# Another order of the head steps and another bank table in a gated delta-rule attention kernel

## The reference, cut to what matters

```
qkvz = x @ W_qkvz ; q, k, v go through a causal convolution of 4 taps and silu
q, k are normalised; each of 16 key heads serves 2 value heads (32 in all, width 128)
for every token t, for every value head:
    S = S * exp(g_t);  delta = (v_t - k_t S) * beta_t
    S = S + k_t delta; o_t = q_t S
out = (silu(z) * rms_norm(o) * norm_w) @ W_out
experts: 12 dense experts (256 -> 640 -> 256) with a top-3 mask, then an early-exit factor
```

## Time and profile before

| what | us |
|---|---|
| median of 3 runs (1511.14 to 1515.55) | 1513.2 |
| the profiled execution, its own time | 1513.14 |
| its span in the profile | 1511.4 |
| PE, DVE, ACT, POOL busy in the span | 1422.6, 1129.0, 1060.1, 704.5 |

### The profile page before, as it was taken

One profiled execution on the slowest core, in us unless ns is written; L12 is line 12 of the kernel. 1 busy time (PEld: TensorE's weight loads), 2 busy tenths in 40 slices (PEclk: granted clock), 3 DMA queues, 4 the chain that ended last, 5 costly groups with the idle time before them and its releaser, 6 DMA issues.

```text
span 1511.4 us, 38181 instructions
## 1 busy us (share of the span) xinstructions
PE 1422.6 (94%) x15004; PEld 1133.0 (75%) x15004; DVE 1129.0 (75%) x1992; ACT 1060.1 (70%) x2136; POOL 704.5 (47%) x619
## 2 busy tenths in 40 slices
PE   5679999999999999999999999999877999999995
PEld 3459888897888889888888888888853465665675
DVE  5579999999999999999999999998765421221224
ACT  6467887878788887878888787887646646546430
POOL 0535545455554544555545455544327534435330
PEclk9799999999999999999999999999999899999997
DMA  3000203112020211202021120302330211111100
GB/s 115 1 1 23 57 2 58 23 37 36 23 58 2 58 23 37 36 23 58 9 51 31 29 37 22 57 13 33 69 77 31 70 36 36 59 47 36 36 1 29
DMA packets 101000, 55.92 MB, mean 37 GB/s; under 512 B 74572, under 2 KB 93016, under 8 KB 100824
## 3 DMA queue, kind: packets, MB, share of 16 engines
q1 hardware_dynamic: 100824, 53.47, 14.8%
HBM read 35.62 MB, written 1.05 MB: 24 GB/s over the span
## 4 chain that ended last, share of the span: by engine, by line
PE 70%; DVE 9%; issue 7%; POOL 5%; ACT 5%; DMA 4%; DVEq 0%; SPq 0%; POOLq 0%; ACTq 0%
PE bank L387 8%; PE bank L1327 8%; PE bank L1311 7%; PE bank L542 5%; PE bank L588 4%; PE bank L559 4%; PE bank L529 3%; PE bank L577 3%; PE bank L568 3%; DVE con L878 3%; DMA sqo<-oo 3%; PE bank L469 2%; ACT h L1427 2%; PE bank L477 2%; PE bank L485 2%
## 5 line engine op out<-in xcount | busy, mean ns | idle before, releaser
L878 DVE SCALAR_TENSOR_TENSOR con<-bank,taps,con 128x1022 f32<-128x1022 f32 (+2 forms) x192 | 245.4, 1278 | 13.0 <-ACT con L657 8.4
L1633 POOL TENSOR_TENSOR h<-h 128x512 f16<-128x512 f32 x120 | 147.4, 1231 | 162.6 <-ACT h L1427 155.5
L1034 POOL TENSOR_TENSOR gl<-const_sb,gc 128x512 f16<-128x512 f32 x128 | 129.6, 1039 | 144.2 <-DVE gc L888 84.3
L387 PE MATMUL bank<-x,qkv 128*128 128x512 f16 x768 | 184.5, 392 | 10.8 <-DVE con L878 10.8
L1311 PE MATMUL bank<-y,w 128*128 128x512 f16 x720 | 170.2, 387 | 10.8 <-ACT h L1427 8.1
L1426 ACT ACTIVATE h<-bank,b 128x512 f32<-128x512 f32 x120 | 82.4, 687 | 122.0 <-PE bank L1311 120.2
L1327 PE MATMUL bank<-w,h 128*128 128x256 f16 x1440 | 162.9, 276 | 1.7 <-DVE facc L1542 1.2
L1327 PEld LDWEIGHTS bank<-w,h 128*128 128x128 f16 x1440 | 141.6, 99 | 23.5 <-DVE facc L1542 3.6
L1311 PEld LDWEIGHTS bank<-y,w 128*128 128x128 f16 x720 | 64.1, 99 | 112.1 <-ACT h L1427 47.7
L387 PEld LDWEIGHTS bank<-x,qkv 128*128 128x128 f16 x768 | 73.2, 100 | 93.3 <-issue 12.3
L936 DVE TENSOR_TENSOR X<-X,bank 128x512 f16<-128x512 f16 x192 | 129.6, 682 | 15.2 <-PE bank L477 13.4
(11 more groups left out here) (217 smaller groups left out, 3924.3 us busy)
## 6 DMA issues: line engine op xcount, KB each, us to landing
w<-in_w SPq DMA_DIRECT2D x24, 640.0 KB, 4.5
w_qkv<-in_W_qkvz SPq DMA_DIRECT2D x16, 512.0 KB, 3.9
w_z<-in_W_qkvz SPq DMA_DIRECT2D x16, 256.0 KB, 2.8
w_out<-in_W_out SPq DMA_DIRECT2D x16, 256.0 KB, 3.0
Z<-in_xT SPq DMA_DIRECT2D x2, 512.0 KB, 5.7
y<-in_x SPq DMA_DIRECT2D x1, 1024.0 KB, 8.1
sqo<-oo SPq DMA_TRANSPOSE x64, 3.1
out_dram<-y SPq DMA_DIRECT2D x8, 128.0 KB, 1.8
```

Of the source, the lines that this page charges most:

```text
L387: last = mm(bank[:, b], qkv16[:, w, a, t * P:(t + 1) * P], x16[:, x, a, b * S:(b + 1) * S], start=(a == k == 0), stop=(a == HT - 1 and k = ...
L878: stt(out=out, in0=bank[:, 0:B, 0:S - k], scalar=taps[:, par, t, TAPS - 1 - k:TAPS - k], in1=out, op0=ALU.mult, op1=ALU.add).then_inc(tap_ ...
L1034: last = tt(gl[:, g % 2, k].rearrange("p (m r) d -> p m r d", m=2), upper.unsqueeze(1).unsqueeze(1).broadcast_to([P, 2, R, P]), gc[:, par, ...
L1633: tt(h16[:, n % 3, 1, t, at], h32[:, k % H32], h16[:, n % 3, 0, t, at], ALU.subtract).then_inc(h_low, 1)
```

## The change

ORDER has the same 167 steps in another sequence. Six of them belong to another head relative to the walk: `once`(1), `res`(3) go from a = 0 to 1; `gl`(2), `decay`(0), `decay`(1) from 2 to 1; the load of w_qkv from 2 to 3. BANK is another table. Every instruction keeps its shape and operands. The five bank constants of the gates and the experts change too, and the walk in which the gate steps come last is now named (-2) since the deepest is now -3; that walk holds only the load for head 0, which is issued ahead of the walks in both kernels.

```
-    (1, "kk", 0), (1, "load", "z"), (1, "aT", 0), (1, "kk", 1),
+    (1, "decay", 0), (0, "Z", 2), (1, "kk", 0), (1, "kk", 1),
...
-GATE_BANKS = (4, 2)
+GATE_BANKS = (6, 2)
+GATE_WALK = -2
 DEEP = max(a for a, *_ in ORDER)
...
-    if w > -DEEP:
+    if w != GATE_WALK:
         return ORDER
...
-H_BANKS = (3, 5)
-LOGIT_BANK, SUM_BANK = 4, 6
-O_BANKS = (2, 7)
+H_BANKS = (3, 4)
+LOGIT_BANK, SUM_BANK = 6, 7
+O_BANKS = (5, 2)
```

More of the change, by code:

```diff
@@ L39 @@
 ORDER = [
[11 rows of a table removed]
-    (1, "aH", 3), (2, "load", "qkv"), (1, "turn", (0, 0)), (1, "unit", 3),
[10 rows of a table removed]
[L62 to L67, removed]
@@ L68 @@
-    (1, "y", (5, 0)), (1, "p", (3, 1)), (2, "tap", 2), (2, "sq1", 1),
-    (0, "weigh", 0), (2, "tok", 0), (2, "tok", 1), (1, "turn", (4, 0)),
[5 rows of a table removed]
[L75 to L79, removed]
@@ L80 @@
-    (1, "res", 2), (1, "Z", 0), (1, "once", 2), (1, "kd", 1),
-    (2, "silu", 0), (1, "aL", 3), (0, "op", 2), (2, "decay", 1),
+    (1, "decay", 0), (0, "Z", 2), (1, "kk", 0), (1, "kk", 1),
+    (1, "aT", 0), (1, "gl", 2), (1, "pT", 0), (1, "unit", 0),
+    (0, "split", "z"), (1, "unit", 1), (1, "decay", 1), (0, "Z", 1),
+    (1, "v", (1, 0)), (1, "aT", 1), (0, "solve", 0), (0, "once", 3),
+    (0, "oT", 0), (1, "kk", 2), (1, "pT", 1), (0, "su", 0),
+    (2, "split", "qkv"), (1, "aH", 0), (1, "aL", 0), (1, "decay", 2),
[7 rows of a table added]
@@ new lines @@
+    (1, "load", "out"), (1, "unit", 2), (1, "turn", (0, 0)), (1, "y", (1, 0)),
[6 rows of a table added]
+    (1, "turn", (0, 1)), (1, "p", (2, 0)), (0, "pdl", 2), (0, "sqo", 1),
+    (1, "p", (1, 1)), (1, "y", (3, 0)), (2, "tap", 2), (0, "sum", 1),
+    (0, "sum", 2), (2, "sq1", 1), (2, "tok", 0), (2, "tok", 1),
+    (0, "sqo", 2), (0, "solve", 3), (1, "turn", (2, 0)), (2, "silu", 2),
[6 rows of a table added]
+    (0, "power", 0), (0, "weigh", 0), (1, "turn", (4, 0)), (1, "turn", (3, 1)),
+    (0, "low", 0), (0, "high", 0), (0, "high", 1), (0, "weigh", 1),
@@ new lines @@
+    (1, "y", (4, 1)), (0, "z", 2), (1, "p", (5, 0)), (0, "z", 3),
+    (1, "p", (4, 1)), (2, "tap", 3), (0, "weigh", 2), (1, "turn", (5, 0)),
+    (2, "gl", 0), (2, "v", (0, 0)), (0, "weigh", 3), (1, "load", "z"),
+    (1, "y", (5, 1)), (0, "low", 1), (1, "turn", (4, 1)), (3, "load", "qkv"),
+    (1, "res", 0), (1, "res", 1), (2, "kT", 0), (0, "high", 2),
+    (0, "low", 2), (1, "once", 0), (0, "op", 0), (2, "silu", 3),
+    (0, "low", 3), (0, "high", 3), (2, "proj", 0), (1, "p", (5, 1)),
+    (0, "op", 1), (1, "Z", 0), (1, "kd", 1), (2, "tap", 0),
@@ L82 @@
+    (1, "turn", (5, 1)), (1, "once", 1), (1, "res", 2), (1, "res", 3),
+    (0, "op", 2), (2, "gl", 1), (1, "once", 2), (2, "silu", 0),
     (0, "op", 3),
@@ L85 @@
 BANK = {
[11 rows of a table removed]
-    ("solve", 3): 7, ("turn", (3, 0)): 3, ("decay", 0): 4, ("y", (3, 1)): 2, ("pdl", 3): 7,
-    ("p", (4, 0)): 6, ("turn", (2, 1)): 5, ("norm", 0): 3, ("y", (5, 0)): 4, ("p", (3, 1)): 7,
-    ("tok", 0): 6, ("tok", 1): 5, ("turn", (4, 0)): 2, ("z", 0): 3, ("z", 1): 4,
[3 rows of a table removed]
-    ("once", 0): 2, ("p", (5, 1)): 5, ("res", 1): 7, ("op", 1): 6, ("turn", (5, 1)): 5,
-    ("res", 2): 4, ("Z", 0): 3, ("once", 2): 5, ("op", 2): 2, ("decay", 1): 5,
-    ("op", 3): 7,
-}
-GATE_BANKS = (4, 2)
[10 rows of a table added]
+    ("tok", 0): 5, ("tok", 1): 3, ("solve", 3): 4, ("turn", (2, 0)): 2, ("qs", 3): 6,
[5 rows of a table added]
+    ("turn", (4, 1)): 4, ("res", 0): 2, ("res", 1): 3, ("kT", 0): 6, ("once", 0): 4,
+    ("op", 0): 7, ("p", (5, 1)): 4, ("op", 1): 6, ("Z", 0): 2, ("turn", (5, 1)): 5,
+    ("once", 1): 3, ("res", 2): 4, ("res", 3): 6, ("op", 2): 5, ("once", 2): 3,
+    ("op", 3): 2,
+}
+GATE_BANKS = (6, 2)
+GATE_WALK = -2
 DEEP = max(a for a, *_ in ORDER)
```

## The result

The changed kernel takes 1543.95 us (median of four runs, 1535.63 to 1548.76) against 1512.17 for the kernel before on the same chip: a ratio of 1.0208, 95% interval 1.0169 to 1.0246. It is slower, as forecast, by 32 us where 19 were forecast. The profiled execution took 1548.76 us, with a span of 1546.9: 35.5 more than before. Two executions among those of the variants fell in a slow state (`first_loads`, 8173 us; `sum_and_sqo`, 1554.9 us) and count in no ratio.

What follows compares the result with a forecast made beforehand. DVE's program-order row was taken to hold PE mid-walk: 65.66 - 0.71 + 2.4 = 67.35 us per walk, +23.7 for 14 walks; with -4 and -0.6, +19.1. Forecast 1532 us, own range 1522 to 1545, overall 1515 to 1550.

Steps and rivals of the forecast that it cites:

- (1): Mid-walk, pdl(2) to p(5,1): DVE's row needs 26.06 us against PE's 23.64, so PE stands still 2.4 us per walk.
- the remark on ACT in the bounds: Upper bound 3.4 us if ACT's sq1 ahead of solve(3) and the bank y(2,1) takes came on top; expected to hide.
- (2): PE's waits for ACT's aH at st and for the transposes at op both go: -0.7 us per walk, between -0.9 and 0.
- (3): f32 steps following an fp16 one, 0.06 us more each, go from 22 to 21 per walk: nothing.
- (4): Fill, walk -1: first projection comes 11 us earlier among the levels; -4 us, between -9 and +2.
- (5): Drain: walk 14 unchanged, 2 us to either side; walk 15 gains 0.6 us from earlier Z(3) and once(3); experts 0.
- A: Rival: POOL and DVE block each other at the weighs, 0.7 to 2 us per walk, about 1550 us; chance 0.12.
- B: Rival: DVE stretch doesn't bind, only removed waits, fill and the 0.6 count; 1498 us; chance 0.07.
- C: Rival, no change: PE waits only at its first place, 1.0 us per walk, fill gives 9 us; 1507 to 1515; chance 0.08.
- D: Rival: walk also longer through transposes and ACT, +1 us per walk beyond the forecast, 1546 us; chance 0.08.

Runs made afterwards that it cites:

- first_loads: Changed kernel with the 32-column norm and the loads of w_z, w_qkv and w_out all ahead of oT(0); ratio 1.0227 to the kernel before.
- sum_and_sqo: Changed kernel with sqo(1) and sum(1) earlier, sqo(2) behind turn(2,0), and the 32-column norm; ratio 1.0129 to the kernel before, median 1534.4 us.
- b_su_first: Kernel before with su(0) moved ahead of st(0), which waited for aH; ratio 0.9973, median 1506.2 us.
- extra_stretch: Changed kernel with the 32-column norm and one more 0.60 us DVE reduction per walk ahead of y(2,1); ratio 1.0245 to the kernel before, median 1549.9 us.
- late_sqo2: Changed kernel with sqo(2) on ACT moved behind turn(2,0); ratio 1.0198 to the kernel before, clean walk 67.25 us.
- early_loads: Changed kernel with the 32-column norm and the loads of w_z and w_qkv moved behind that of w_out; ratio 1.0231 to the kernel before, median 1547.7 us.
- wide_norm: Changed kernel with norm(0)'s eight matmuls writing 32 columns each instead of one; ratio 1.0185 to the kernel before, median 1540.1 us.

## Why the prediction was right, step by step

**(1) The DVE stretch: right in its sum.** +2.4 was forecast and 2.40 measured; a clean walk of 67.35 was forecast and is 67.25. That the walk came so near has a part of luck. Its base, 64.95, took off 0.71 us of waits, in which the wait for the transposes is counted in two rows. The old order without the wait for `aH` has a clean walk of 65.10 (b_su_first), and from there the sum gives 67.50; the new order is 2.15 us longer and not 2.4. Where the other 0.25 us are won, outside the stretch, is not shown. extra_stretch shows that the row binds to the last tenth. What failed is the place, and the remark on ACT in the bounds came nearer than the text above it: the first 1.1 us fell on y(2,1), for ACT, and not on the third `proj`. late_sqo2 shows that they are one debt: what is paid at the one isn't due at the other. That y(2,1) takes the bank of solve(3) comes from the new bank table; no run changes the order or the table alone. The sum did not tell, either, how little a repair would bring: three limits lay within 0.5 us of each other, and that made two expectations of mine too large by 0.24 and one by over 1 us.

**(2) The removed waits: half right.** The one for `aH` went; b_su_first prices it at 0.30 us per walk. The transposes were taken as late no more, and this step failed: `op`'s matmuls waited 3.3 us in 4 walks, against 2.2 in 4 before. The 6.2 us in 11 times of the earlier trace rows, on which the 0.71 rests, are 2.2 of the matmuls and 4.0 of the weight loads. Loads behind the last transpose, which the prediction held against it, were not shown to be the reason: early_loads shows the harm of loads ahead of one, and the late landings are there without any.

**(3)** can't be told apart from 0 in these rows.

**(4) The fill: wrong.** -4 was forecast, +0.6 measured. The first `proj` was early by 11 us (66.08 against 76.94), but from the third to the fourth it took 16.3 us instead of 9.3. Here the stretch before, then after:

```profile
94.69:103.98 9.29, 7.97 (x72) 4.97 (x73) 6.88 (x9) 5.47 (x10) 1.93 (x2) 0.82 0.00 0
```

```profile
90.33:106.66 16.33, 13.97 (x192) 9.69 (x193) 12.17 (x18) 9.92 (x18) 8.23 (x8) 0.83 0.00 1
```

The new order has 192 matmul records between the two, the old one 72: what was taken out ahead of the first `proj` stands ahead of the last, and the step that counted the first alone failed. In the chain of waits one `proj` there took 5.30 us at the lower clock, not the 4.5 that I allowed.

**(5) The drain.** Walk 14 +2.1, at the end of the 2 us allowed. Without the four `proj` the levels of the new order stand closer: PE waits 1.27 ahead of st(2) and 1.28 ahead of y(1,1), which have 2.6 us of `proj` just before them in a full walk. Walk 15 came out unchanged and not 0.6 shorter. Experts: +0.7.

**The rest of the miss: disturbance.** 9.8 us in the walks against 3.7 before. Two falls of the clock make 3.8 of it, the four walks with late transposes (1, 3, 5 and 10) 4.0, walk 0 1.6. The forecast took the clock as staying at 1.00; in this order it fell in six walks of 56, and with wide_norm in none. The account of the spans: +19.1 forecast; the walks 8.3 more (-1.4 for clean walks of 67.25, +9.8 for disturbance, of which the forecast had none), the fill 4.6, walk 14 2.1, walk 15 0.7, the experts 0.7: +35.5. Between the medians it is 31.8, and 1543.95 us lies near the upper end of the forecast's own range.

**The rivals.** A fell at the weighs: they last 1.13 us beside `low` too. POOL was the one to pay there:

```profile
572.71 1.33 POOL L1070 TENSOR_TENSOR oo<-oo 128x512 f16<-128x512 f32 x1 [1.92 <-ACT oo L786]
...
576.00 1.16 POOL L1070 TENSOR_TENSOR oo<-oo 128x512 f16<-128x512 f32 x1
```

The first `low` begins in the last 0.3 us of weigh(1) and takes 1.33; one that meets none takes 1.16. So the meeting costs 0.17 us, on the engine that has time. By the Trainium skill, "SBUF — State Buffer", section "SBUF: two separate sides", whichever of the two starts first has the port pair for its whole instruction, and the other waits. One instruction of a weigh starts 0.26 us after the one before, and these rows fit that rule: the weigh was there first and `low` waited, for no longer than that. At `aT` POOL is first, and DVE pays:

```profile
524.60 1.27 POOL L1043 TENSOR_TENSOR pT<-kkm,decay 128x512 f32<-128x512 f32 x1 [0.52 <-ACT decay L707]
```

```profile
525.27 1.14 DVE L916 TENSOR_TENSOR aT<-kkm,decay 128x512 f32<-128x512 f32 x1
```

The median `aT` of the full walks is 1.12 us, before it was 0.69. So the rival was right that the two engines meet more in the new order, and wrong on the place: this is ahead of pdl(2), where DVE has pauses of 0.86 and 1.10 us in walk 6, and not in the row that binds. B and C fell with the walk. D's time, 1546, is nearest to the result. Of its ground, late transposes are a part of the disturbance, but a clean walk is not 1 us longer than forecast.

## What to carry to other kernels

Lay the program order of the waiting engine beside that of the engine waited for, and sum both between two fixed points: that gave the cost of an order to 0.1 us in 26. Then sum for every limit that ends at the same point (the row, the bank, the single dependency), since the gain from a repair is only the distance to the next one. Read a wait of TensorE for the matmuls and the weight loads apart, or the same event counts twice. A wait seen in a profile is a place where a debt is paid, not its cause: the largest one here was worth nothing alone and 0.51 us once the row beside it was short, while 0.26 us of another were worth 0.30.

## What the runs showed of the hardware

The granted clock fell to 1.2 GHz (0.58 on the mean of 3.4 us from 618.73) in the middle of a full walk, with PE busy all through it. Ahead of it stood 16 fp32 matmuls of one column, 1.92 us long; with 32 columns they last as long, 1.95 us, and no fall followed in 70 walks. Where the old order has the same matmuls, none followed either, in four traces.
